# Layers of a transformer on one core: attention with the value and output weights folded, scores one step ahead

## What is computed

```python
for i in range(6):
    x = attn_layer(shift_tokens(x), Wqkv[i], q_scale[i], k_scale[i], Wo[i]) + x
    x = ffn_layer(shift_tokens(x), ...) + x
# attn_layer, 16 heads of 64, windows of 32 tokens:
q, k, v = split(x @ Wqkv)              # 3 x 1024 columns
q, k = l2norm(q) * qs, l2norm(k) * ks  # then a rotary turn of each
sim = 8 * q_w . k_(w-1, w)             # 32 queries, 64 keys: own window and the one before
out = softmax(mask(sim)) @ v_(w-1, w)
return concat_heads(out) @ Wo
```

## Time and profile before

| | |
|---|---|
| median of 3 runs | 2913.63 us (2913.45 to 2914.07) |
| profiled execution, first to last instruction | 2911.7 us |
| layers, start to end | 1163 to 2912 us |
| TensorE busy | 96% |
| VectorE, ScalarE, GpSimd busy | 80%, 60%, 58% |
| TensorE's granted clock | 0.996 of 2.4 GHz |

### The profile page before, as it was taken

How to read it: one execution, slowest core, us unless ns; L and a number is a source line. 1 busy time by engine, 2 the same in 40 slices (tenths; PEclk the granted TensorE clock), 3 DMA queues, 4 the chain that set the end, 5 groups by cost and what they waited for, 6 DMA issues and landing times.

```text
span 2911.7 us, 98296 instructions
## 1 busy us (share of the span) xinstructions
PE 2789.5 (96%) x40886; PEld 1832.5 (63%) x40886; DVE 2336.3 (80%) x3830; ACT 1746.4 (60%) x2618; POOL 1680.3 (58%) x1454
## 2 busy tenths in 40 slices
PE   8999999999999999899999999999999999999997
PEld 5556565655665655566656666666666666666665
DVE  6777755774677776998968999889998999898884
ACT  4455555555666665556666666666666666666663
POOL 1000002000466665676767888878887888788882
PEclk9999999999999999999999999999999999999999
DMA  3000000000011111243234434333443343333332
GB/s 97 1 1 1 1 1 3 1 1 10 21 45 46 45 46 31 77 129 79 73 103 106 99 86 114 84 93 88 114 95 91 92 118 91 88 89 83 89 85 66
DMA packets 183114, 188.24 MB, mean 65 GB/s; under 512 B 77517, under 2 KB 130515, under 8 KB 181139
## 3 DMA queue, kind: packets, MB, share of 16 engines
q1 hardware_dynamic: 182675, 181.94, 24.8%
HBM read 61.00 MB, written 6.03 MB: 23 GB/s over the span
## 4 chain that ended last, share of the span: by engine, by line
PE 73%; DVE 10%; issue 5%; POOL 5%; SPq 3%; ACT 3%; DMA 1%; DVEq 0%; POOLq 0%; ACTq 0%
PE ps L1348 13%; PE ps L587 13%; PE ps L1356 5%; PE ps L1400 5%; PE ps L1442 4%; PE ps L1363 4%; PE ps L622 4%; PE ps L600 4%; PE ps L1389 2%; PE ps L1456 2%; PE ps L1409 2%; PE ps L534 2%; PE ps L605 2%; PE ps L1457 2%; DVE nmx L695 2%
## 5 line engine op out<-in xcount | busy, mean ns | idle before, releaser
L1348 PE MATMUL ps<-wqkv,xcT 128*128 128x512 f32 x1152 | 553.2, 603 | 4.7 <-DVE area L1886 1.6
L587 PE MATMUL ps<-xnT,qp 128*128 128x512 f32 (+3 forms) x1280 | 527.1, 543 | 17.2 <-ACT prob L814 16.3
L2030 POOL TENSOR_TENSOR ra<-ra,rb 128x1024 f32<-128x1024 f32 x191 | 452.4, 2375 | 121.9 <-DVE rb L1854 121.0
L814 ACT ACTIVATE prob<-ps,ebias,shift 128x1024 f32<-128x1024 f32 (+7 forms) x384 | 360.3, 955 | 124.0 <-DVE ebias L704 60.4
L822 ACT ACTIVATE probT<-ps 128x512 f32<-128x512 f32 (+3 forms) x384 | 207.9, 541 | 353.6 <-PE ps L600 353.5
L587 PEld LDWEIGHTS ps<-xnT,qp 128*128 128x128 f32 x1280 | 231.7, 191 | 273.6 <-issue 228.5
L2049 POOL TENSOR_TENSOR ra<-ra,rn 128x1024 f32<-128x1024 f32 x192 | 362.3, 1908 | 8.9 <-DVE ra L1946 1.2
L695 DVE TENSOR_REDUCE nmx<-ps 128x1 f32<-128x1024 f32 (+7 forms) x256 | 245.8, 987 | 108.3 <-PE ps L587 93.3
L1348 PEld LDWEIGHTS ps<-wqkv,xcT 128*128 128x128 f32 x1152 | 196.7, 190 | 154.3 <-issue 143.5
L1630 ACT ACTIVATE sq<-ps 128x1024 f32<-128x1024 f32 x192 | 195.6, 1019 | 85.6 <-PE ps L1348 85.3
L1852 DVE TENSOR_TENSOR ra<-ps,tab 128x1024 f32<-128x1024 f32 x192 | 233.6, 1217 | 3.7 <-issue 3.1
(11 more groups left out here) (274 smaller groups left out, 5651.9 us busy)
## 6 DMA issues: line engine op xcount, KB each, us to landing
vw<-vs SPq DMA_DIRECT2D x576, 130.0 KB
vw<-vs SPq DMA_DIRECT2D x384, 65.0 KB
bc<-bc_scratch SPq DMA_DIRECT2D x128, 128.0 KB, 2.9
area<-bc_scratch SPq DMA_DIRECT2D x128, 128.0 KB, 4.3
wqkv<-lwqkv_dram SPq DMA_DIRECT2D x6, 1536.0 KB, 8.6
xc<-xs SPq DMA_DIRECT2D x96, 32.0 KB
wo<-lwo_dram SPq DMA_DIRECT2D x6, 512.0 KB, 9.6
xc<-xs SPq DMA_DIRECT2D x96, 31.8 KB
```

The source lines that it names most:

```text
L587: mm = E.matmul(ps[:, 2 * r + o // 512, 0:w], k.qp[:, group % 2, g % NTH * P:(g % NTH + 1) * P], k.xnT[:, k0 + o:k0 + o + w], start=True, ...
L814: A.activation(k.prob[:, r, 0:nk], ps[:, 2 * r:2 * r + 2, :].rearrange("p a b -> p (a b)")[:, 0:nk], ACT.Exp, bias=k.ebias[:, row % 2:row ...
L1348: mm = E.matmul(to[:, c, :], k.xcT[:, n % 4, :], k.wqkv[l % 2][:, at + 512 * c:at + 512 * (c + 1)], start=True, stop=True)
L2030: G.tensor_tensor(k.ra[:, n % 2, w, :], k.ra[:, n % 2, w, :], k.rb[:, w, :], ALU.add).then_inc(s("added_" + what), 1)
```

## The change

The values are no longer computed. For each head the value weights and the output weights are multiplied once per layer (`fold`, twelve pieces in all, `wvo`), the probabilities of a head act on the tile's own input (`mix`: 32 tokens of input as weights, 16 heads x 32 queries as moving columns), and the output product runs over 16 heads of 128 in place of 8 pairs of heads. The input tile is kept in a ring of eight, and `keys_before` copies it shifted by a window. VectorE sums the exponentials, multiplies by the reciprocal and transposes in blocks of 32x32 (`weigh`), so TensorE turns neither probabilities nor outputs. VectorE shifts only the second bank of scores, in PSUM; ScalarE takes the first bank's exponentials in eight pieces with the maximum as bias, and the second bank's in one. A rotation is one product of 2048 elements, and its sum on GpSimd is two halves. The scores of tile n+1 are computed in step n, around the mix. The output bias of the feed-forward part goes into the down product as one more row. The copies behind each scan go to ScalarE, the scans to the end of VectorE's step, the units to one step later, and the convolution's pieces to steps 4 to 14.

```diff
@@ pair_table
+    x, y, z, w = 0, 3, 2, 1
     for n in range(LAST_STEP):
-        a, b, c, d = (3, 1, 2, 0) if n % 2 else (0, 1, 2, 3)
...
+        table.update({("q", n + 2): x, ("k", n + 2): y, ("side", n): z, ("rows_q", n + 1): x, ("rows_k", n + 1): y, ("late", n): z, ("extra", n): z,
+                      ("scores", n + 1): x, ("mix0", n): w, ("mix1", n): y})
...
+        x, y, z, w = z, w, y, x
@@ transformer_pe
+    def fold(place, n, l, half):
+        to = pair((place, n), ("folded", 2 * l + half + 1))
+        E.wait_ge(s("wvo"), 32 * (l + 1))
+        for j in range(4):
+            for o in range(2):
+                at = slice(o * DH, (o + 1) * DH)
+                mm = E.matmul(to[:, o, j * P:(j + 1) * P], k.wvT[at, 4 * half + j, :], k.wo[at, 4 * half + j, :], start=True, stop=True, skip_group_check=True)
+        mm.then_inc(s("fold_mm"), 1)
+
+    def mix(n):
+        to = [pair((f"mix{i}", n), ("mixT", 2 * n + i + 1)) for i in range(2)]
+        E.wait_ge(s("prT"), n + 1)
+        E.wait_ge(s(f"xp{n % PRING}"), 32 * (n // PRING + 1) - (0 if n % PRING else 16))
+        prT = k.prT[:].rearrange("p (c a q) -> p c a q", a=2, q=WIN)
+        for half in range(2):
+            for w in range(4):
+                at = slice(WIN * w, WIN * (w + 1))
+                of = k.xc[at, n % XRING, :] if half == 0 else k.xp[at, n % PRING, :]
+                mm = E.matmul(to[w // 2][:, w % 2, :], of, prT[at, :, 1 - half, :], start=half == 0, stop=half == 1, skip_group_check=True)
+                if half == 1 and w % 2 == 1:
+                    mm.then_inc(s("mixed"), 1)
@@ side
-            for c in range(8):
-                mm = E.matmul(to[:, 0, 0:P], k.oT[:, c * P:(c + 1) * P], k.wo[:, l % 2, c, :], start=c == 0, stop=c == 7, skip_group_check=True)
+            for c in range(H):
+                mm = E.matmul(to[:, 0, 0:P], k.mixT[:, c, :, :].rearrange("p w q -> p (w q)"), k.wvo[:, l % 2, c, :], start=c == 0, stop=c == H - 1, skip_group_check=True)
@@ transformer_act
+    def probs(n, o):
+        of = pair("scores", n)[:, o, :]
+        if o == 0:
+            A.wait_ge(s("top_s"), n + 1)
+            for j in range(8):
+                here = of[:, j * DH:(j + 1) * DH]
+                ins = A.activation(here, here, ACT.Exp, bias=k.nmxl[:, n % 2, j:j + 1])
+        else:
+            A.wait_ge(s("shifted_s"), n + 1)
+            ins = A.activation(of, of, ACT.Exp)
+        ins.then_inc(s("exp"), 1)
@@ transformer_dve
+    def weigh(n):
+        V.wait_ge(s("exp"), 2 * n + 2)
+        V.tensor_reduce(k.suml[:], heads("scores", n), X_AXIS, ALU.add).then_inc(s("v"), k.v.up())
...
+        V.reciprocal(k.recl[:], k.suml[:]).then_inc(s("v"), k.v.up())
...
+        V.tensor_tensor(k.pr[:].rearrange("p (h d) -> p h d", d=DH), heads("scores", n), bcast(k.recl[:], 2, DH), ALU.mult).then_inc(s("weighed"), 1)
...
+        V.transpose(k.prT[:], k.pr[:]).then_inc(s("prT"), 1)
...
-        V.tensor_tensor(out_a, of, bcast(tab[:, 2 * w, :], 1, H), ALU.mult)
-        V.tensor_tensor(out_b[:, :, 0:32], of[:, :, 32:64], bcast(tab[:, 2 * w + 1, 0:32], 1, H), ALU.mult)
-        V.tensor_tensor(out_b[:, :, 32:64], of[:, :, 0:32], bcast(tab[:, 2 * w + 1, 32:64], 1, H), ALU.mult).then_inc(s("rotated_" + what), 1)
...
+        V.tensor_tensor(k.rot[:, n % 2, w, :, :].rearrange("p c (h d) -> p c h d", d=DH), bcast(heads(what, n), 1, 2),
+                        bcast(k.tab[:, n % FRAME, 2 * w:2 * w + 2, :], 2, H), ALU.mult).then_inc(s("rotated_" + what), 1)
@@ transformer_pool
-        G.tensor_tensor(k.ra[:, n % 2, w, :], k.ra[:, n % 2, w, :], k.rb[:, w, :], ALU.add).then_inc(s("added_" + what), 1)
+        G.tensor_tensor(a[:, :, 0:DH // 2], a[:, :, 0:DH // 2], b[:, :, DH // 2:DH], ALU.add)
+        G.tensor_tensor(a[:, :, DH // 2:DH], a[:, :, DH // 2:DH], b[:, :, 0:DH // 2], ALU.add).then_inc(s("added_" + what), 1)
```

More of the change, by code:

```diff
@@ L44 @@
 SCANS = 9060
[L45 to L46 removed]
+XRING, PRING = 8, 4
 class Count:
@@ L1599, in transformer_pe @@
             rates(n, RATE_STEPS[n])
+        for place, l, half in FOLDS.get(n, ()):
+            fold(place, n, l, half)
+        forward(n)
+        if n == HAT_STEP:
+            turn_hat()
+        if n in IN_EXTRA:
+            project_in("extra", n, IN_EXTRA[n])
+        if n + 1 < NTILE:
+            scores_first(n + 1)
         if n < NTILE:
-            turn_out(n)
-        if n == NTILE - 1:
-            forward(n)
+            mix(n)
+        if n + 1 < NTILE:
+            scores_second(n + 1)
 def transformer_act(k):
@@ L1819, in heads, with top, shift @@
         return pair(*key).rearrange("p a (h d) -> p (a h) d", d=DH)
[L1821 to L1824 removed]
+    def top(n):
+        V.wait_ge(s("lscore"), n + 1)
+        V.tensor_reduce(k.nmxl[:, n % 2, :], heads("scores", n), X_AXIS, ALU.max, negate=True).then_inc(s("top_s"), 1)
+    def shift(n):
+        here = pair("scores", n)[:, 1, :].rearrange("p (h d) -> p h d", d=DH)
+        V.wait_ge(s("top_s"), n + 1)
+        V.tensor_tensor(here, here, bcast(k.nmxl[:, n % 2, H // 2:H], 2, DH), ALU.add).then_inc(s("shifted_s"), 1)
@@ L1990, in transformer_dve @@
             normalise_last()
-        if n == NTILE + 6:
-            down_last()
-        elif n % 4 == 2 and m >= 1:
-            down(m - 1)
-        elif what and what != "turn_normal" and not gate_first:
-            gated(m, int(what[2]))
         if n == NTILE + 3:
@@ L2003, in transformer_dve @@
             add_layer(2)
+        for u in units(n + 1):
+            scan(u)
 def transformer_pool(k):
@@ L2324 @@
     qs, ks = a["L1_ffn_q_scale"], a["L1_ffn_k_scale"]
-    turned = lambda v: np.concatenate([v[:, DH // 2:], v[:, :DH // 2]], 1)
-    by_heads = lambda v, axis, order: np.concatenate([np.take(v, range(DH * h, DH * h + DH), axis) for h in order], axis)
     b1 = np.zeros((L, P, 6), np.float32)
```

436 lines of the change are left out of this document (176 added, 260 removed).

## The result

| | before | after |
|---|---|---|
| median of the runs (4 each) | 2913.85 us | 2835.36 us |
| lowest to highest | 2913.45 to 2916.93 | 2830.42 to 2836.46 |
| profiled span | 2911.7 us | 2833.4 us |

The ratio is 0.9728, with the interval 0.9714 to 0.9741: 2.7% faster. The forecast was 2800, range 2730 to 2895, faster at 0.88. The range held, and the kernel stands 35 us above the number forecast.

The account below looks back on a forecast made before the run. TensorE bounds the layer steps at 17.28 of 17.65 us. With TensorE at 15.8, VectorE at 15.7 and 0.7 idle, steps take 16.4; gains of 101, 9 and 2 us give 2800 us, range 2730 to 2895.

Parts of the forecast that it names:

- TensorE, goes and comes: TensorE's work per layer step: 5.27 us goes; 1.78, 1.9 for the mix and 0.1 for folds come; 17.28 becomes 15.8.
- the serial mix: Rival: the mix's matmuls on TensorE run one after the other, 7.3 us, kernel 3290; chance 0.09 for slower.
- the one by pairs: Within the rival of no overlap: two array quarters of the mix at a time, 3.7 us, kernel 2945.
- VectorE: VectorE's work per late step: savings against 3.85 us of new weighing, net -0.1, so it stays at 15.7 us.
- upper end 2.6: VectorE's 32x32 transposition in the weighing: taken as 1.2 us, at most 2.6, from one SBUF addition of 1024 elements.
- The coupling term: Idle time from TensorE and VectorE waiting for each other: 0.7 us a step, 0.37 before, giving steps of 16.4.
- the other 81 steps gain 1.25: All layer steps after step 14 fall from 17.65 to 16.4 us, 101 us together.
- it stays at 15.0: GpSimd's work per step: halved additions cost about 0.2 us more a pair, a bias addition goes; total 15.0 us.
- Steps 0 to 14 and the tail: Steps 0 to 3 unchanged, steps 4 to 14 gain 0.8 us each, 9 together; the tail loses 2 us.
- Closer coupling: Rival: idle time stays 0.37 us a step and the mix takes its lower end; 2760; chance 0.15 for below 2765.
- Looser coupling: Rival: queue waits of 1.5 us a step or a slow transposition, 2860 to 2880; chance 0.25 for 2840 to 2907.
- A step set by a third engine, GpSimd: Remainder of the last rival: GpSimd at 15.0 us plus its waits sets the step, 16.5, the forecast's own figure.

Follow-up runs that it names:

- clamp_reduce: Changed kernel with the lower bound on the sums of squares taken by a reduction over pairs again: 2804.04 us, 0.964 of the kernel before.
- rate_last: Changed kernel with `rate` placed behind the rotation sums in GpSimd's step: 2813.97 us, 0.9674 of the kernel before.
- rc_none: Changed kernel with reduction clamp and `rate` behind rotation sums, plus no VectorE shift, ScalarE taking 16 biased exponentials: 2785.34 us, 0.9562 of the kernel before.
- act_normal: `rc_none` with every fourth step's normalisation moved from GpSimd to ScalarE as four activations with scale and bias: 2785.49 us, 0.9587 of the kernel before.

## Why the prediction was right, and where it was not

**TensorE, goes and comes: right but for the folds.** The mix was put at 1.9 us and takes 1.93; the serial mix (7.3) and the one by pairs (3.7) are excluded, and so is the 2.4 us worked out from the packing section of the Trainium skill's "TensorE: Matmul & The Clock Gate" (3.07 for four row tiles; here 7.3/1.93 is 3.8). TensorE's sum came to 562.25/36.4 = 15.4 us a step against 15.8 (36.4 steps of 16.479 us in the stretch). The folds were sized as matmuls only, 0.1 us a step. Their matmuls take 1.16 us each, 0.15 a step, and their place costs 17.2 us of waiting for ScalarE's copies, 0.18 a step more, which the sum did not hold.

**VectorE: right by its terms, with one missing.** Transposition 1.25 (taken 1.2, upper end 2.6), rotation 2.2 by starts, weighing as summed. The busy time is 579.06/36.4 = 15.9 against 15.7. The sum left the clamp as it was, 0.22, and it became another instruction, which waits for GpSimd. It costs 0.53 us more, and mending it gave 0.33 a step, 26 us in all. So the other terms came out 0.3 below their sum. The trace of the kernel before had such a wait to read: the 2.6 us that the prediction took as the upper end for the transposition is one addition from 1174.32 to 1176.93 us, begun while GpSimd was at work:

```profile
1173.95 1.90 POOL L2049 TENSOR_TENSOR ra<-ra,rn 128x1024 f32<-128x1024 f32 x1
```

GpSimd ended at 1175.85, and the addition 1.08 us later.

**The step: 16.48 against 16.4.** The coupling term was 0.7 us idle on TensorE; it is 16.48 - 15.4 = 1.0. So the two errors on TensorE nearly cancel, 0.35 too much work and 0.33 too little idle, and that is luck; of the idle time 0.18 a step is the folds'. In the table, the prediction's 1.25 a step became 1.107: the step before was taken as 17.65 and is 17.586 by these marks, and the step after is 0.08 longer than forecast. This shortfall is not spread evenly. The 16 steps that begin with the folds (24 to 27, 40 to 43, 56 to 59, 72 to 75) gained 0.78 each and the other 53 gained 1.20, so 7.5 of the 10 us are missing in the steps with the folds and behind them. That the folds' place is the cause is read from the trace and has no run of its own. With the clamp mended (`clamp_reduce`) the same two groups gain 0.96 and 1.58: the clamp's wait is in both, and without it the 53 steps gain more than the 1.25 forecast. GpSimd is at 15.2 (said 15.0), ScalarE at 12.6 (said 13), its eight small exponentials at about 0.21 each (eight in 1.72 us).

**Steps 15 to 22: wrong.** The step that failed is "the other 81 steps gain 1.25": it treats steps 15 to 22 like the late ones. On GpSimd I counted durations (two halves for one sum, "it stays at 15.0") and not the order: the norms ahead of `rate` had changed from tile n+2 to n+1, which took away the wait that had covered ScalarE's activations. It came back as 25.7 us in two waits in front of the sums, and TensorE's lower clock behind them adds to it. `rate_last` gives 16.6 of the 19 us back in its profile, and 16 us by its ratio.

**Before the loop: 6.6 us not costed.** The folds are not in it; the first two stand in step 0, from 1196.95 us. TensorE turns the first rows late, waiting 3.06 us for GpSimd's norms:

```profile
1178.12 3.54 PE L1360 MATMUL ps<-ident,rot 128*128 128x128 f32 x16 [3.06 <-POOL rot L2038]
```

These 16 turnings take 3.54 us in place of 2.03, and eight projection records behind them 5.40 in place of 3.70; the granted clock from 1175 to 1192 us is 0.80. A gap of 2.30 us in the scores has no cause in the trace, and the keys' projection of tile 2 now lies ahead of the mark. No run takes these apart.

**Steps 0 to 14 and the tail: right** (10.5 and 7 us against 9 and 7). `rc_none` shows that VectorE is the bound of the early steps, as the prediction read from the earlier trace rows.

**The rivals.** Closer coupling did not come. Looser coupling with a slow transposition did not either; the time ended between forecast and that rival, 5 us from its 2840, which is a coincidence: that figure rests on a slower mix, and the mix took 1.93 us. "A step set by a third engine, GpSimd" is not what holds the changed kernel, where GpSimd has 3% of the chain; with the clamp mended it has 29%, and `act_normal` does not settle it. GpSimd also sets time through VectorE's instructions, which no rival said.

## What to carry to other kernels

When a change brings three engines within a few per cent of each other, add up the engines' sums as usual, then read each instruction that waits for another engine and ask what is queued behind it: the wait in `rate`, the clamp and the copy of a fold were each one instruction in front of a full queue. Where an instruction lasts several times what its size would cost, as the clamp did, look at what ends at the same moment: it may be waiting, though it counts as busy. Before removing or moving small work, ask what it keeps apart: taking four 32-element operations off GpSimd cost 2.7%.
